# Row maxima of the attention scores: four heads a tile of 32-row products in place of two heads a tile of 64-row products

## The reference, cut to what matters

```python
def step(state, inp):                       # 1024 steps, one after the other
    p_t, g_t = inp
    state = jnp.tanh(p_t + state)
    return (state, g_t * state)
...
q = _rms(heads(wq), qn_w); k = _rms(heads(wk), kn_w); v = heads(wv)     # heads: (B, 16, T, 16)
scores = jnp.einsum('bhqd,bhkd->bhqk', q, k) * HD ** (-0.5)
scores = jnp.where(causal[None, None], scores, -jnp.inf)
attn = jax.nn.softmax(scores, axis=-1)
ao = jnp.einsum('bhqk,bhkd->bhqd', attn, v).transpose(0, 2, 1, 3).reshape(B, T, C) @ wo.T
...
moe = wts[:, 0:1] * o0 + wts[:, 1:2] * o1 + wts[:, 2:3] * o2 + wts[:, 3:4] * o3
```

## Time and profile before

| | before |
|---|---|
| time, median of 3 runs | 1466.83 us (1464.5 to 1470.28) |
| the profiled execution's own time | 1454.77 us |
| its span | 1453.0 us |
| granted TensorE clock, mean | 0.997 |
| PE busy | 1407.3 us, 97% |
| PEld busy | 1169.3 us, 80% |
| DVE busy | 1096.2 us, 75% |
| ACT busy | 883.7 us, 61% |
| POOL busy | 312.7 us, 22% |

### The profile page before, as it was taken

The page is one execution under the profiler, slowest core; times in us unless marked ns, Lnnn a source line. Parts: engine busy times, 40 slices in busy tenths (PEclk is TensorE's granted clock), DMA queues, the critical chain, the costliest instruction groups (busy, mean ns, idle before and its releaser), DMA issues.

```text
span 1453.0 us, 35319 instructions
## 1 busy us (share of the span) xinstructions
PE 1407.3 (97%) x13160; PEld 1169.3 (80%) x13160; DVE 1096.2 (75%) x2916; ACT 883.7 (61%) x2262; POOL 312.7 (22%) x1146
## 2 busy tenths in 40 slices
PE   9999899999999999999999999999999999999997
PEld 6478789978997688877988689867887677986797
DVE  7858777566899877778998788788899378772544
ACT  3546577567666774776676952468322886339841
POOL 3344333332133323333333200001000100001100
PEclk9999999999999999999999999999999999999999
DMA  3547766765576657646666666676566666667453
GB/s 108 167 146 232 220 209 181 226 215 155 163 230 209 200 180 202 199 141 185 214 202 193 199 199 201 203 222 208 166 194 197 207 214 180 205 207 248 150 172 120
DMA packets 242234, 278.63 MB, mean 192 GB/s; under 512 B 35088, under 2 KB 165648, under 8 KB 241808
## 3 DMA queue, kind: packets, MB, share of 16 engines
q1 hardware_dynamic: 242064, 276.38, 62.5%
HBM read 234.18 MB, written 43.45 MB: 191 GB/s over the span
## 4 chain that ended last, share of the span: by engine, by line
PE 70%; DVE 14%; ACT 6%; DMA 3%; issue 3%; POOL 2%; SPq 1%; ACTq 0%; DVEq 0%; POOLq 0%
PE PS L1563 65%; PE PS L1566 3%; PE PS L1646 2%; POOL AD L2227 2%; DVE mx L2026 1%; ACT PX L1387 1%; DMA KT<-ktd 1%; DVE st L1844 1%; ACT work L1494 1%; DMA QT<-MT 1%; ACT PX L1494 1%; DVE ss L1992 1%; DVE rst L1831 1%; DVE rst L1825 1%; DVE mv L1847 0%
## 5 line engine op out<-in xcount | busy, mean ns | idle before, releaser
L1387 ACT ACTIVATE PX<-AD 128x8 f32<-128x8 f32 x1023 | 221.2, 216 | 217.6 <-POOL AD L2227 210.4
L2227 POOL TENSOR_TENSOR AD<-PX 128x8 f32<-128x8 f32 x1023 | 245.7, 240 | 499.8 <-ACT PX L1387 489.5
L2026 DVE TENSOR_REDUCE mx<-PS 128x2 f32<-128x1024 f32 (+3 forms) x256 | 254.9, 1018 | 40.4 <-PE PS L1563 39.6
L1563 PE MATMUL PS<-EP,u_e_l 128*128 128x256 f32 x1024 | 194.1, 284 | 1.3 <-issue 1.2
L1494 ACT ACTIVATE work<-PS 128x1024 f32<-128x1024 f32 (+1 forms) x199 | 182.2, 958 | 13.3 <-PE PS L1563 12.5
L1563 PE MATMUL PS<-WB,work 128*128 128x192 f32 x1024 | 180.1, 330 | 0.1
L1563 PE MATMUL PS<-work,vlx 128*32 128x256 f32 (+2 forms) x2104 | 174.8, 365 | 4.8 <-ACT work L1494 1.2
L1563 PE MATMUL PS<-EP,WB 128*128 128x256 f32 x640 | 178.8, 279 | 0.0
L1531 ACT ACTIVATE work<-PS 128x512 f32<-128x512 f32 x132 | 77.3, 595 | 160.6 <-PE PS L1563 160.1
L1563 PEld LDWEIGHTS PS<-WB,work 128*128 128x128 f32 x1024 | 164.9, 190 | 3.9 <-ACT work L1531 1.1
L1563 PEld LDWEIGHTS PS<-EP,u_e_l 128*128 128x128 f32 x1024 | 160.2, 188 | 4.5 <-issue 3.1
(11 more groups left out here) (201 smaller groups left out, 2600.7 us busy)
## 6 DMA issues: line engine op xcount, KB each, us to landing
KT<-ktd SPq DMA_DIRECT2D x112, 512.0 KB, 4.4
WB<-wlo_e_l SPq DMA_DIRECT2D x160, 256.0 KB, 3.6
ktd<-KTs SPq DMA_DIRECT2D x32, 512.0 KB, 4.3
WB<-wlo_e_up SPq DMA_DIRECT2D x64, 256.0 KB, 3.9
WB<-wlo_e_w SPq DMA_DIRECT2D x64, 256.0 KB, 3.8
WB<-wdn_e_down SPq DMA_DIRECT2D x64, 192.0 KB, 2.9
KT<-ktd SPq DMA_DIRECT2D x48, 256.0 KB, 3.6
KT<-ktd SPq DMA_DIRECT2D x32, 384.0 KB, 3.6
```

What stands on the lines that cost most here:

```text
L1387: eng.activation(cur, AD[n % 2], ACT.Tanh).then_inc(of(*key), 1)
L1563: return eng.matmul(o, l, r, start=start, stop=stop, skip_group_check=skip)
L2026: eng.tensor_reduce(o, two("mxm", *a)[:, :, 0:w], AX, ALU.max, negate=True).then_inc(of(*key), 1)
L2227: eng.tensor_tensor(AD[n % 2], PX[c % 2][:, :, :, t], PX[(n - 1) // L % 2][:, :, :, (n - 1) % L], ALU.add).then_inc(of(*key), 1)
```

## The change

One `mxm` tile now holds four heads. The low parts leave the 32 rows that the first pass reads, so a head's product takes 32 rows, and four heads stand in the 128 partitions as four row tiles. The tile is four products into two pairs of banks (`P2` and `P2b`), which need not be neighbours. The masks of a tile are sixteen products of 32 columns (`pick` by `stair`). Tiles fall from 384 to 192, of which 128 have masks; the streamed columns fall from 147,456 to 73,728. `mxr` stays at 384 reductions of the same shapes, two to a tile. `kh` writes its copy and its difference in two halves each, `qq` its difference. The constants on GpSimd take more steps. The keys of stages 2 and 3 are loaded as two planes by up to 512 keys instead of one plane by all keys: as many transfers (96 for `ktm`), as many bytes. The list `MB` of at most four open tiles is gone. The maxima go to other rows of the queries, with two transfers as before.

All order tables are new: `mxm` stands in 174 runs, 164 of them of one tile; TensorE's items change their tiling 744 times (the first pass no longer shares a tiling with `sc`); `WARM` holds 405 fillers. `STEPS` has 2545 other items before the last step of the recurrence, where it had 2636; in both, 120 `up` and 32 `dn` items and half of the first pass's tiles (192 of 384, 96 of 192) stand after it.

```diff
-BANKS = {"P2": 2, "P1": 1}
+BANKS = {"P2": 2, "P2b": 2, "P1": 1}
...
 def jobs_of(u):
-    return [(g, (0, 1)) for g in range(4)] if u < 2 * B else [(g, (pl,)) for g in range(4) for pl in range(2)]
+    return [(g, h) for g in range(4) for h in range((key_blocks(u) + 3) // 4)]
...
-                take = {"P2": (("mxr", u, i),), "MB": (("mxr", u, i),)}
+                take = {"P2": (("mxr", u, i, 0),), "P2b": (("mxr", u, i, 1),)}
...
                     for par in range(2):
-                        rows = slice(64 * par, 64 * par + 64)
-                        ins = mm(ps[:, par, 0:w], qt[rows, 2 * g + pl, 128 * s:128 * s + 128], kt[rows, pl - planes[0], k0:k0 + w],
-                                 True, True)
+                        for pl in range(2):
+                            rows = slice(64 * par + 32 * pl, 64 * par + 32 * pl + 32)
+                            ins = mm(tile[pl][:, par, 0:w], qt[rows, 2 * g + pl, 128 * s:128 * s + 128], kt[rows, pl, 0:w], True, True)
                     if diag < w:
-                        for i in range(2):
+                        for i in range(4):
                             for par in range(2):
-                                rows = slice(64 * par, 64 * par + 64)
-                                ins = mm(ps[:, par, diag + 64 * i:diag + 64 * i + 64], pick[rows, i, :],
-                                         (maskq, maskn)[i][rows, 64 * par:64 * par + 64], False, True, True)
+                                for pl in range(2):
+                                    rows = slice(64 * par + 32 * pl, 64 * par + 32 * pl + 32)
+                                    ins = mm(tile[pl][:, par, diag + 32 * i:diag + 32 * i + 32], pick[rows, i, :], stair[rows, :],
+                                             False, True, True)
...
-                    step(eng.tensor_copy(pair, x.unsqueeze(2).to_broadcast([128, 16, 2, 16])))
-                    v.wait_ge(link, steps[0])
-                    eng.tensor_tensor(QKP[:, :, low:low + 16], x, QKP[:, :, 0:16].bitcast(F32), ALU.subtract).then_inc(of(*key), 1)
+                    if kind == "kh":
+                        for pl in range(2):
+                            step(eng.tensor_copy(
+                                QKP[:, 8 * pl:8 * pl + 8, 32 * pl:32 * pl + 32].rearrange("p h (r d) -> p h r d", r=2),
+                                x[:, 8 * pl:8 * pl + 8, :].unsqueeze(2).to_broadcast([128, 8, 2, 16])))
...
+                    for pl in range(2):
+                        hs = slice(8 * pl, 8 * pl + 8)
+                        ins = eng.tensor_tensor(QKP[:, hs, low[pl]:low[pl] + 16], x[:, hs, :],
+                                                QKP[:, hs, high[pl]:high[pl] + 16].bitcast(F32), ALU.subtract)
...
-                    eng.tensor_reduce(o, two("mxm", *a)[:, :, 0:w], AX, ALU.max, negate=True).then_inc(of(*key), 1)
+                    eng.tensor_reduce(o, (two, far)[pl]("mxm", u, i)[:, :, 0:w], AX, ALU.max, negate=True).then_inc(of(*key), 1)
```

More of the change, by code:

```diff
@@ L110 @@
[L110 to L115, removed]
@@ L555, in __init__ @@
     def __init__(self):
-        self.items, self.after, self.queue = {}, {}, set()
+        self.items, self.after, self.queue, self.fresh = {}, {}, set(), set()
     def add(self, engine, key, us, *after, seq=(), take=None, mode=None, kb=0.0):
@@ L662, in run @@
                     t = max(t, t1)
+                if k in self.fresh and after == k[0]:
+                    us += RELOAD
                 us *= clock(t)
@@ L786, in arrange @@
     add("pool", ("ident",), 1.4, take={"PT": gated, "EF": split})
-    add("pool", ("consts",), 6.6, ("ident",), take={"PT": gated, "EF": split})
+    add("pool", ("consts",), 11.6, ("ident",), take={"PT": gated, "EF": split})
     for n in range(T):
@@ L845, in arrange @@
         ends = {j: max(i for i, t in enumerate(tiles) if t[0] == j) for j in range(len(jobs))}
-        for j, (g, planes) in enumerate(jobs):
-            dma(("ktm", u, j), 64 * len(planes) * nkb * two, *keys, seq=before("ktm"), n=two, take={"KT": (("mxm", u, ends[j]),)})
+        for j, (g, h) in enumerate(jobs):
+            blocks = min(4, nkb - 4 * h)
+            dma(("ktm", u, j), 128 * blocks * two, *keys, seq=before("ktm"), n=two, take={"KT": (("mxm", u, ends[j]),)})
             prior["ktm"] = (u, j)
-            for i, (j_, s, pl, k0, w) in enumerate(tiles):
+            for i, (j_, s, k0, w) in enumerate(tiles):
                 if j_ != j:
                     continue
-                take = {"P2": (("mxr", u, i),), "MB": (("mxr", u, i),)}
+                take = {"P2": (("mxr", u, i, 0),), "P2b": (("mxr", u, i, 1),)}
+                P.fresh.add(("mxm", u, i))
                 if i == 0:
@@ L1060, in two, with far @@
             return PS[:, i:i + 2, :]
+        def far(*key):
+            i = place[key, "P2b"]
+            return PS[:, i:i + 2, :]
         def one(*key):
@@ L1312, in _ @@
                         sp.wait_ge(*x)
-                    kt, n = KT[place[key, "KT"]], 128 * key_blocks(u)
+                    kt, n = KT[place[key, "KT"]], min(512, 128 * key_blocks(u) - 512 * h)
                     if u < B:
@@ L1325, in _ @@
                     sp.wait_ge(*latest([("mxm", u, i) for i in range(len(tiles_of(u)))]))
-                    for par in range(2):
-                        eng.dma_start(plain(qt[48 + 64 * par:49 + 64 * par, :, :]),
-                                      plain(MT[8 * par:8 * par + 8, :])).then_inc(of(*key), 16)
+                    for pl in range(2):
+                        row = (48, 16)[pl]
+                        eng.dma_start(plain(qt[row:row + 65:64, pl:8:2, :]), plain(MT[8 * pl:8 * pl + 8, :])).then_inc(of(*key), 16)
                 elif kind == "kts":
@@ L1572, in _ @@
                         pe.wait_ge(*x)
+                if (key, "P2b") in place:
+                    for x in freed(key, "P2b"):
+                        pe.wait_ge(*x)
                 if (key, "P1") in place:
@@ L2018, in _ @@
+                    v.wait_ge(link, steps[0])
+                    for pl in range(2):
+                        hs = slice(8 * pl, 8 * pl + 8)
+                        ins = eng.tensor_tensor(QKP[:, hs, low[pl]:low[pl] + 16], x[:, hs, :],
+                                                QKP[:, hs, high[pl]:high[pl] + 16].bitcast(F32), ALU.subtract)
+                    ins.then_inc(of(*key), 1)
                 elif kind == "mxr":
[L2019 to L2020 removed]
+                    u, i, pl = a
@@ L2034, in _ @@
                     v.wait_ge(*done("mtr", u))
-                    eng.tensor_scalar(MT, one("mtr", u)[0:16, 0:256], 1.0, None, ALU.add).then_inc(of(*key), 1)
+                    eng.tensor_copy(MT, one("mtr", u)[0:16, 0:256]).then_inc(of(*key), 1)
                 elif kind == "avc":
@@ new lines, in _ @@
+                    for i in range(4):
+                        step(eng.affine_select(out=pick, in_=pick, compare_op=ALU.not_equal, fill=1.0, base=-32 * i,
+                                               pattern=[[0, 4], [0, 128]], channel_multiplier=1))
+                        pool.wait_ge(clink, steps[0])
+                    step(eng.affine_select(out=pick, in_=pick, compare_op=ALU.is_ge, fill=0.0, base=-1,
+                                           pattern=[[32, 4], [-1, 128]], channel_multiplier=0))
@@ L2212, in _ @@
+                    pool.wait_ge(clink, steps[0])
+                    o = bass.AP(pick.tensor, pick.offset, [pick.ap[0], [160, 4], [1, 31]])
+                    for i in range(4):
+                        step(eng.affine_select(out=o, in_=o, compare_op=ALU.not_equal, fill=1.0, base=-32 * i - 1,
+                                               pattern=[[0, 4], [-1, 31]], channel_multiplier=1))
+                        pool.wait_ge(clink, steps[0])
                     step(eng.affine_select(out=maskk, in_=maskk, compare_op=ALU.is_ge, fill=BIG, base=0,
```

312 lines of the change are left out of this document (155 added, 157 removed), and 711 rows, old and new, of tables (PINNED, PLACES, STEPS, WARM).

## The result

The changed kernel takes 1480.19 us (median of 7 runs, 1478.83 to 1487.35), the kernel before 1466.83 in the same session: ratio 1.0095 [1.0078, 1.0112]. The change costs 14 us, where 20 us of gain were forecast, and the time lies 11 us above the range. The profiled execution took 1478.83 us. Parts of a trace are therefore also compared with those of other kernels that share that part.

The account below looks back on a forecast made before the run. TensorE was taken to bound the kernel from 353 us on. -30.7 - 8.6 + 15.8 + 1 + 3.3 = -19.2 us against the profiled 1454.8, plus 12.1 to the median, gave 1447 us, range 1427 to 1469.

Parts of the forecast that it names:

- Columns and fixed parts of the tiles: First pass on TensorE: fewer streamed columns save 30.7 us, smaller fixed parts of tile runs save 8.6 us.
- rivals 1 and 3: Four row tiles slow each other, 1456 us, chance 0.12; their weight loads go one after the other, 1488 us, chance 0.09.
- The mask rounds: Masks of a first-pass tile: four rounds taken at 0.04 us each, with -10 to +20 us possible overall.
- Changes of tiling: TensorE's queue: 744 changes of tiling instead of 665, at 0.20 us each, lose 15.8 us.
- From 353 us on TensorE sets the pace, and what is saved on it there is saved in the span.: From 353 us to the end: TensorE bounds the kernel, so its savings there count in full.
- Rival 2: Banks and VectorE replace TensorE as the limit: 1466 us, chance 0.14; sign: waits for maxima of 20 us and more.
- The prediction's own sign of being wrong in kind: Whole kernel: if tiles cost what was forecast and the span still doesn't fall, TensorE wasn't the bound.
- Stage 0: Up to 353 us, where the recurrence has a say: half of a sixth of 39.3 us is lost, 3.3 us.
- The clock: TensorE's granted clock: taken as 1.00, the 2.4 GHz level, 0.417 ns a column.
- (c), four banks for a tile: First-pass tiles waiting for two pairs of banks: taken as 0, between -4.7 and +19 us.
- VectorE's splits: 96 more VectorE instructions: 0 to 13.6 us more work there, 1 us taken on the path.
- Constants on GpSimd, key loads: More GpSimd selects end before the recurrence's first addition; key loads keep number and bytes: no cost for either.

Follow-up runs that it names:

- (2): Changed kernel with each 32-row product issued twice: 1500.56 us, 1.0240; changed kernel's order with the old form, two 64-row rounds a tile: 1516.41 us, 1.0351.
- the typical execution: Profiled execution, 1462.53 us, of the kernel before with only 21 recurrence steps moved ahead of ScalarE items; that kernel's ratio is 0.9995.
- (6): Kernel before with the tanh of recurrence steps 300 to 399 computed twice, the second waiting for the first: 1483.48 us, 1.0119.
- (4, by medians): Recurrence steps moved ahead of waiting ScalarE items: 47 in the changed kernel, 1473.50 us, 1.0070; 21 in the kernel before, 1463.63 us, 0.9995.
- (5): Changed kernel with 65 more fillers at 12 places: 1474.56 us, 1.0073; with these and 47 recurrence steps moved ahead of ScalarE items: 1473.55 us, 1.0076.
- (7): Each first-pass reduction over only the first half of its keys: kernel before 1461.14 us, 0.9954; changed kernel 1467.06 us, 1.0013.
- (3): New form in the order of the kernel before, each pair of old tiles made one four-head tile at the later's place: 1574.13 us, 1.0735.

## Why the prediction was wrong, point by point

- *Columns and fixed parts of the tiles, -30.7 and -8.6 us.* Right as work on TensorE: 134 to 93 us (2), tiles within 0.04 us of forecast. Four row tiles run together and load together, so rivals 1 and 3 are out. The mask rounds were no dearer than forecast (0.108 us for sixteen products, 0.544 less 0.436, against 0.16). The 0.11 us between loads that the prediction reads as those of one round (1200.64 and 1200.75 in the earlier trace rows) lies between loads of two whole products; no term of the sum hangs on it. The rule of the Trainium skill ("TensorE: Matmul & The Clock Gate", "Part 3: Packing small matmuls — row/col tiling") that four products of 32 rows gain only 3.07 times would have made the mask-free tile 0.42 + 0.3 x 0.213 = 0.48, as an estimate; it takes 0.44. The traces don't bear it out here, and a second round alone adds 1.09 times its columns (2).
- *Changes of tiling, +15.8 us for 79.* The trace has 57 more (731 to 788), 27 of them the form's (the old form in the new order has 761). In sum the second stretch's work fell by 16.6 us, about as the terms would have it. The price of 0.20 us for a change was not tested by itself.
- *"From 353 us on TensorE sets the pace, and what is saved on it there is saved in the span."* **This step failed.** It nearly holds for the kernel before (0.81 for one, idle time unchanged). It was carried over to another order, in which TensorE is idle for 19.1 us more after the 512th step (16.1 against the typical execution): its work there fell by 17 to 18 us and the stretch by at most 2. Rival 2's sign, waits for the maxima of 20 us, didn't show: they rose from 4.7 to 8.6. In the second stretch no single releaser holds the new idleness: waits for ScalarE's `work` went from 2.6 to 5.1 us, for the maxima from 3.4 to 4.4, for values from 0.3 to 1.5, and waits for `WB` weights of `dn` (1.9) and for ScalarE's `UU` (1.6) are new. It was priced nowhere, because only the table's tiling changes were counted as the cost of a new order. The prediction's own sign of being wrong in kind came (tiles cost what it said, the span didn't fall); its reading of that sign, that TensorE wasn't the bound, is true of the new order more than of the old.
- *Stage 0: "3.3 us are taken back; at the ends 0 and 6.6".* **The second failed step, and the larger in its size.** The first 353 us were asked only how much of a gain they would pass on, never whether they could get longer. They did, by 21 us between the two traces and by 17.9 against the typical execution. The other kernels with old order and old form reach the 512th step at 356 to 358 us; the changed kernel, and with its products issued twice, at 373 to 374, without masks at 369, with the old form at 379. What this lateness is worth at the end differs by the order: 0.84 to 1.0 for one in the old (6), less than half in the new (4, by medians). The term itself was also mis-sized: stage 0 has one sixth of the tiles but one twelfth of the columns, so half of its share is 2.0 us, not 3.3.
- *The clock.* Taken as 1.00 throughout. It fell before the 373rd us in six places, after or in waits of TensorE. Few fillers give back some 3 us, with overlapping intervals (5). Before the 512th step the old form in the new order was at half clock for 44.6 us (2), the changed kernel for 47.6, so nearly all of this is the order's.
- *(c), four banks for a tile, 0 of 0 to 19.* Too low: some 5 us by (7), barely clear of nothing, and 65 us of waits in the old order (3). Rival 2 had the mechanism but not the place: by (7) it bites before the 512th step, where it delays the recurrence, and hardly from there on.
- *VectorE's splits, 0 to 13.6 us.* 8.2 us of work more (1096.2 to 1104.4). *Constants on GpSimd, key loads:* hidden, as said.

Together: the new form took some 40 us of work from TensorE, and the order that it needs gave all of it back and 14 us more. The loss lies ahead of the 512th step (17.9 to 21.3 us later), and behind it nothing is left of the saving that was forecast (1103.5 us against 1100.8 and 1105.2). Edits that act on the clock, on ScalarE's waits and on the reductions each bring the 512th step 8.5 to 9.8 us forward, overlapping, but give 3.2, 3.7 and 12.1 us at the end: lateness at that step and loss at the end are not one thing in the new order. What stays open is which of the new order's placements make TensorE idle on either side of the 512th step, and how much of the second stretch is the clock. Of the versions tried one beats the kernel before, its own with half reductions (7), which leaves work out.

## What to carry to other kernels

A saving on the bounding engine is worth about its face value only while the order around it stays (0.81 here, some half of it in the new order); a price found in one order need not hold in another, and the same may go for the price of lateness. When every table is new, ask of each stretch whether it can get longer, the one paced by another chain first. In-order queues turn one engine's lateness into another's: an item placed just ahead of a serial chain's step is safe only as long as its producer is on time. A product that takes half of PSUM at once may need an order made for it, and that order is part of its price. And a single trace of a kernel can be 12 us off its median: set beside it the trace of a near twin before reading differences of a few microseconds from it.

## What the runs showed of the hardware that was not expected

- Four products of 32 rows start and load together, and a mask-free tile of four heads and 512 keys takes 0.436 us of TensorE's queue, with sixteen masks 0.544 (medians).
- A second round of four such products adds 0.232 us to a tile of 0.436, 1.09 times its columns (run 2).
- The granted clock halved nine times ahead of the kernel's end though TensorE is 95% busy, each time in or after waits whose longest was 0.9 to 5.5 us, for 3.4 to 13.7 us. Raising it to 0.998 with 260 fillers did not shorten the kernel; that the fillers took what the clock gave is likely, and not shown.
- Six reductions of 128 x 1024 in a row hold VectorE for 7 us while TensorE waits 1.71 us for a bank:

```profile
1131.45 2.35 DVE L2019 TENSOR_REDUCE mxb<-PS 128x2 f32<-128x1024 f32 x2
1133.72 4.61 DVE L2019 TENSOR_REDUCE mx<-PS 128x2 f32<-128x1024 f32 x4
...
1135.08 0.51 PE L1538 MATMUL PS<-KT,QT 32*128 32x512 f32 x4 [1.71 <-DVE mx L2019]
```
